# Reordering the convolution chunk on TensorE and splitting the bias out of the low-rank matmul, in an eight-core S4 + mixture-of-LoRA layer

## The reference

```python
x = _layernorm(x + s4(x))      # s4: causal convolution along the 4096 features, plus D*x
x = _layernorm(x + ffn(x))
# ffn:
base_out  = einsum('bsi,oi->bso', x, W) + b
gates     = softmax(einsum('bsi,ei->bse', x, Wr))
proj_r    = einsum('bsi,eri->bser', x, A)
lora_out  = einsum('bser,eor->bseo', proj_r, Bm)
out       = base_out + einsum('bse,bseo->bso', gates * 2.0, lora_out)
```

## Time and profile before

| | us |
|---|---|
| median of 2 runs | 1901.37 |
| the two runs | 1819.21 and 1983.53 |
| the profiled execution | 1824.94 |
| its span, core 1, the slowest | 1823.9 |
| spans of all cores | 1786.8 to 1823.9 |
| TensorE matmul busy | 1368.1 (75%) |
| ScalarE, VectorE busy | 298.3, 354.3 |

### The profile page before, as it was taken

The page is one execution under the profiler, slowest core; times in us unless marked ns, Lnnn a source line. Parts: engine busy times, 40 slices in busy tenths (PEclk is TensorE's granted clock), DMA queues, the critical chain, the costliest instruction groups (busy, mean ns, idle before and its releaser), DMA issues.

```text
span 1823.9 us, 15473 instructions; the slowest of 8 cores (1786.8 to 1823.9 us)
## 1 busy us (share of the span) xinstructions
PE 1368.1 (75%) x5820; PEld 558.2 (31%) x5820; DVE 354.3 (19%) x608; ACT 298.3 (16%) x588; POOL 58.8 (3%) x82
## 2 busy tenths in 40 slices
PE   0155547529978767678999996799999687999960
PEld 0024531103333322122444431234444122444420
DVE  2331000033000000516100041531000506200025
ACT  0032326200000000550000035200000550000000
POOL 3000001000000000000000000000000000000000
PEclk9999999857989888897999998799999997999985
DMA  4101024960999994162625405163452152734204
GB/s 84 15 5 12 1 13 55 195 165 1 201 207 204 209 204 128 24 208 102 267 92 202 121 1 148 83 253 139 162 172 59 24 208 76 247 139 161 116 1 184
DMA packets 72911, 222.81 MB, mean 122 GB/s; under 512 B 10820, under 2 KB 60068, under 8 KB 68453
## 3 DMA queue, kind: packets, MB, share of 16 engines
q0 software_dynamic: 58528, 154.10, 35.6%
q1 hardware_dynamic: 14310, 67.73, 9.7%
HBM read 205.32 MB, written 67.43 MB: 150 GB/s over the span
## 4 chain that ended last, share of the span: by engine, by line
PE 60%; DMA 13%; DVE 9%; another core or an unknown queue 7%; ACT 5%; issue 4%; POOL 1%; SPq 0%; DVEq 0%; ACTq 0%; POOLq 0%
PE ps L974 42%; DMA wtb<-WT 7%; DMA uTb<-uT 2%; PE ps L979 2%; ACT r1b L110 2%; DVE nt L105 2%; DVE r1b L105 2%; PE ps L906 1%; DVE bnbuf L105 1%; DMA o<-outf 1%; PE ps L810 1%; PE ps L841 1%; PE ps L848 1%; PE ps L854 1%
## 5 line engine op out<-in xcount | busy, mean ns | idle before, releaser
L974 PE MATMUL ps<-wtb,r1b 128*128 128x512 bf16 x3968 | 897.5, 385 | 60.2 <-DVE wtb L105 60.2
L974 PEld LDWEIGHTS ps<-wtb,r1b 128*128 128x128 bf16 x3968 | 382.8, 99 | 542.7 <-issue 115.3
L110 ACT CAST scr<-ps 128x512 bf16<-128x512 f32 x64 | 37.5, 586 | 968.5 <-PE ps L979 801.4
L105 DVE CAST scr<-ps 128x512 bf16<-128x512 f32 x64 | 44.3, 691 | 572.1 <-PE ps L979 568.7
L105 DVE BATCH_NORM_STATS2 bnbuf<-scr 128x6 f32<-128x512 bf16 x128 | 88.8, 694 | 13.8 <-DVE scr L105 0.7
L110 ACT ACTIVATE uTb<-r1b 128x512 bf16<-128x512 bf16 x128 | 80.6, 629 | 12.8 <-ACT r1b L110 1.5
L110 ACT CAST r1b<-ps 128x512 bf16<-128x512 f32 x128 | 75.0, 586 | 43.7 <-PE ps L856 34.4
L810 PE MATMUL ps<-r1b,onescb 128*1 128x512 bf16 x64 | 24.7, 386 | 74.0 <-DMA uTb<-uT 38.7
L105 DVE TENSOR_TENSOR wtb<-wtb,eyeb 128x128 bf16<-128x128 bf16 x32 | 7.2, 225 | 360.3 <-DMA wtb<-WT 357.5
L938 PE MATMUL ps<-wtb,r1b 128*128 128x512 bf16 x128 | 53.8, 587 | 27.2 <-DVE r1b L105 27.2
L105 DVE TENSOR_SCALAR outf<-scr,bnagg,sigcol 128x1024 f32<-128x1024 bf16 x64 | 52.0, 813 | 111.1 <-DMA o<-outf 108.9
(11 more groups left out here) (597 smaller groups left out, 827.9 us busy)
## 6 DMA issues: line engine op xcount, KB each, us to landing
wtb<-wscr POOLq DMA_DIRECT2D x24, 4096.0 KB, 15.4
wtb<-WT POOLq DMA_DIRECT2D x8, 4096.0 KB, 46.7
wscr<-wtb SPq DMA_DIRECT2D x8, 4096.0 KB, 19.0
o<-outf SPq DMA_DIRECT2D x64, 512.0 KB, 2.8
uTb<-uT POOLq DMA_DIRECT2D x16, 1024.0 KB, 14.5
g<-cvb_re POOLq DMA_DIRECT2D x1, 1024.0 KB, 7.3
g<-cvb_im POOLq DMA_DIRECT2D x1, 1024.0 KB, 10.2
catb<-CatA POOLq DMA_DIRECT2D x1, 288.0 KB, 9.0
```

Of the source, the lines that this page charges most:

```text
L105: t = sy.inc("V", fn(*a, **kw))
L110: t = sy.inc("S", fn(*a, **kw))
L974: T.matmul(ps[bi][0:128, 0:512], r1b[:, it * TT + tb * 128: it * TT + (tb + 1) * 128], wtb[par][:, it * 512:(it + 1) * 512], start=(it == ...
```

## The change

Three edits. (1) In the convolution, the carry-dependent matmuls (`pstat` and both uses of `wout_sb`) go to the end of a chunk's group and wait there for the carry copy of the chunk before; the carry's bank alternates between ps4 and ps5 (`pcb`). (2) The four matmuls for the sums are no longer spread over the next chunk: `st_mm(c-1)` issues them in one piece behind chunk c, behind a wait for all four ScalarE results. (3) The bias is taken out of the 33-row matmul: it becomes a matmul of its own (1 row of ones by 512 elements of `biasrb2`) in front of a 32-row one, and `sprojb` lies in the tile `nt`.

```diff
-    BmTd = dti("BmTd", [33, D4])
+    BmTd = dti("BmTd", [32, D4])
...
+        tk_bb = gdma("GS", biasrb2[0:1, :], biasd.ap())
         gdma("GS", onesrb[0:1, :], onesrd.ap())
...
-        sproj2 = sb("sproj2", [33, TT], BF16)
-        sprojb = sproj2[0:32, 0:TT]
+        sprojb = nt[0:32, 0:TT]
-        t_onerow = vch(V.memset, sproj2[32:33, :], 1.0)
...
+            def st_mm(c_):
+                evA, sqA, evB, sqB = stat_dep[c_]
+                deps = [evA, evB, sqA, sqB]
+                sy.waits("T", deps)
+                for k2 in range(2):
+                    mm1 = T.matmul(ps[6][0:1, 0:512], onescb[:, :], r1b[:, dsl],
+                    mm2 = T.matmul(ps[7][0:1, 0:512], onescb[:, :], uTb[:, ssl],
...
+                sy.waits("T", [bank_r.get(("psC", c % 2)), bank_r.get(pcb)])
+                T.matmul(ps[pcb][0:128, 0:512], win_sb[:, 0:128], uTb[:, slA], start=True, stop=False)
+                T.matmul(ps[pcb][0:128, 0:512], win_sb[:, 128:256], uTb[:, slB], start=False, stop=False)
...
+                sy.waits("T", [cv_prev])
+                cmt = sy.inc("T", T.matmul(ps[pcb][0:128, 0:512], pstat[:, :], carry[cur][:, :], start=False, stop=True))
...
                 if c > 0:
-                    st_part(c - 1, 3)
+                    st_mm(c - 1)
...
-                    sy.waits("T", [t_sp, t_onerow])
+                    T.matmul(ps[bi][0:128, 0:512], onesrb[0:1, :],
+                             biasrb2[0:1, os * 512:(os + 1) * 512], start=False, stop=False)
+                    sy.waits("T", [t_sp])
                     lm = T.matmul(ps[bi][0:128, 0:512],
-                                  sproj2[0:33, tb * 128:(tb + 1) * 128],
-                                  bmtb[0:33, os * 512:(os + 1) * 512], start=False, stop=True)
+                                  sprojb[:, tb * 128:(tb + 1) * 128],
+                                  bmtb[:, os * 512:(os + 1) * 512], start=False, stop=True)
```

More of the change, by code:

```diff
@@ L137, in build_nc @@
         ft = sb("ft", [64, 448], F32)
+        biasrb2 = sb("biasrb2", [1, D4], BF16)
         onesrb = sb("onesrb", [1, 128], BF16)
@@ L151, in build_nc @@
         gdma("GS", onescb[:, :], onescd.ap())
+        tk_bb = gdma("GS", biasrb2[0:1, :], biasd.ap())
         gdma("GS", onesrb[0:1, :], onesrd.ap())
-        t_bB = sy.tok("GS")
+        t_bB = tk_bb
         tk_setup = sy.tok("GS")
@@ L690, in build_nc @@
         catb = sb("catb", [128, NCH * 36], BF16)
-        bmtb = sb("bmtb", [33, D4], BF16)
-        sproj2 = sb("sproj2", [33, TT], BF16)
+        bmtb = sb("bmtb", [32, D4], BF16)
         eyeb = sb("eyeb", [128, 128], BF16)
@@ L800, in build_nc @@
             stats_fin = [None, None]
-            def st_part(c_, part):
+            def st_mm(c_):
                 evA, sqA, evB, sqB = stat_dep[c_]
                 first, last = (c_ == 0), (c_ == 15)
[L805 to L817, removed]
+                deps = [evA, evB, sqA, sqB]
+                if first:
+                    deps += [bank_r.get(6), bank_r.get(7)]
+                sy.waits("T", deps)
+                for k2 in range(2):
+                    dsl = slice((2 * c_ + k2) * TT, (2 * c_ + k2 + 1) * TT)
+                    ssl = slice(((2 * c_ + k2) % 16) * TT, ((2 * c_ + k2) % 16 + 1) * TT)
                     mm1 = T.matmul(ps[6][0:1, 0:512], onescb[:, :], r1b[:, dsl],
-                                   start=False, stop=last)
-                    if last:
+                                   start=(first and k2 == 0), stop=(last and k2 == 1))
+                    mm2 = T.matmul(ps[7][0:1, 0:512], onescb[:, :], uTb[:, ssl],
+                                   start=(first and k2 == 0), stop=(last and k2 == 1))
+                    if last and k2 == 1:
                         stats_fin[0] = sy.inc("T", mm1)
[L822 to L828, removed]
+                        stats_fin[1] = sy.inc("T", mm2)
+                    elif k2 == 1:
+                        stats_fin[0] = sy.inc("T", mm2)
+            cv_prev = None
             for c in range(16):
@@ L832, in build_nc @@
                 biA, biB = c % 2, 2 + c % 2
+                pcb = 4 + c % 2
                 slA = slice(((2 * c) % 16) * TT, ((2 * c) % 16 + 1) * TT)
@@ L855, in build_nc @@
                 T.matmul(ps[biB][0:128, 0:512], band0b[:, :], uTb[:, slB], start=False, stop=False)
+                sy.waits("T", [cv_prev])
+                cmt = sy.inc("T", T.matmul(ps[pcb][0:128, 0:512], pstat[:, :], carry[cur][:, :], start=False, stop=True))
+                bank_w[("psC", c % 2)] = cmt
+                amt = sy.inc("T", T.matmul(ps[biA][0:128, 0:512], wout_sb[:, 0:128], carry[cur][:, :], start=False, stop=True))
+                bank_w[biA] = amt
                 bmt = sy.inc("T", T.matmul(ps[biB][0:128, 0:512], wout_sb[:, 128:256], carry[cur][:, :], start=False, stop=True))
@@ L858, in build_nc @@
                 if c > 0:
-                    st_part(c - 1, 3)
+                    st_mm(c - 1)
                 sy.waits("S", [cmt, bank_r.get("carrynxt%d" % nxt)])
-                cv = sch(S.copy, carry[nxt][:, :], ps[4][0:128, 0:512])
-                bank_r["psC"] = cv
-                bank_r[4] = cv
+                cv = sch(S.copy, carry[nxt][:, :], ps[pcb][0:128, 0:512])
+                bank_r[("psC", c % 2)] = cv
+                bank_r[pcb] = cv
                 bank_r["carrynxt%d" % nxt] = cv
+                cv_prev = cv
                 sy.waits("S", [amt, bmt])
@@ L881, in build_nc @@
                     t_sc2 = ln2_scal(t_vc2)
-            for _p in range(4):
-                st_part(15, _p)
+            st_mm(15)
             t_s1 = stats_fin[0]
@@ L1021, in _host_prep @@
         np.asarray(inputs["L0_ffn_Wr"], dtype=f32).T], axis=1))
-    BmTh = np.ascontiguousarray(np.concatenate([
-        np.asarray(inputs["L0_ffn_Bm"], dtype=f32).transpose(0, 2, 1).reshape(32, D4),
-        np.asarray(inputs["L0_ffn_b"], dtype=f32).reshape(1, D4)], axis=0))
+    BmTh = np.ascontiguousarray(
+        np.asarray(inputs["L0_ffn_Bm"], dtype=f32).transpose(0, 2, 1).reshape(32, D4))
     biash = np.ascontiguousarray(np.asarray(inputs["L0_ffn_b"], dtype=f32))
```

## The result

The changed kernel takes 1841.18 us in the median of 11 runs, the kernel before 1819.2 in the median of 10. Each of the two series holds one run in a slower state of the chip (1960.08 and 1983.53 us), and such runs are left out of every ratio and of every mean over timed runs in this document. The ratio is 1.0127, with a 95% interval of 1.0105 to 1.0149: slower by 23 us, give or take 4. The forecast was 1840.0 for the time and +15.1 us for the difference. The time fits and the difference does not: its base, the profiled execution of 1824.94 us, was some 6 us above what the kernel before usually takes, and the sum was short by 8. That the total came within 1.2 us is luck: the high base made up for the short sum.

A forecast was written before the change was run, and what follows sets the result against it. TensorE bounds later tiles' streams, float32 weight loads tile 0's, a TensorE-ScalarE loop with input stops the convolution. Bias +20.3 and +1.6, setup +0.6, order -7.4 sum to +15.1 on 1824.9: 1840.0 us, range 1822 to 1856.

The forecast's parts named there:

- Bias matmul in tiles 1 to 3: Streams of later tiles: 93 token blocks each pay 0.218 us for the added matmul, all on the path, +20.3 us.
- Rival A: Added matmul pays an unhidden weight load at both neighbours, 0.31 us a block, giving 1849 us; chance 0.20.
- rival B: Only the 33-row shape costs 0.1 us each side, so the split-off bias is free, giving 1818 us; chance 0.07.
- Bias matmul in tile 0: Tile 0's stream: weight loads hide the added matmuls of os 1 to 6; os 0 and os 7 pay, +1.6 us.
- failed cover: Tile 0's stream, if weight loads hide none of the added matmuls: 31 x 0.218 = 6.8 us.
- The order in tile 0: Tile 0's convolution: chunks 1 to 4 and chunk 8 go faster and the first weight blocks are queued earlier, -2.4 us.
- The order in tiles 1 to 3: Convolutions: gains count only from chunk 8, partly lost to a colder clock; -1 in tile 1, -2 each in tiles 2, 3.
- The landing of quarter 3: Convolution input load lands 8.6 us after issue, while ScalarE needs 10.7 us for chunks 9 to 11, so stays hidden.
- rival D: Convolution order is worth nothing: quarter 3 comes late after faster chunks 9 to 11, end goes cold; +22.5, 1847 us; chance 0.11.
- a sign of being wrong: In the convolution: the forecast is wrong if quarter 3 holds chunk 12 for over 1 us.
- The setup: Before the first tile: one more load on GpSimd's queue delays ScalarE's first instruction, +0.6 us.
- The base: The profiled execution of the kernel before, 1824.9 us, to which the forecast difference of +15.1 us was added.

## Why the prediction was right or wrong

**Bias matmul in tiles 1 to 3: right.** 20.3 forecast; the streams add 6.5, 6.6 and 6.9 us, 20.0. The step from the 1-row to the 32-row matmul is 0.23 us. Rival A (0.31) and rival B (no changes of shape) are out: a block takes 7.55, and 128 to 1 and 32 to 128 rows pay 0.1 each like 128 to 33 did.

**Bias matmul in tile 0: the step that failed.** "The loads of blocks 3 to 7 run one after another and hide what os 1 to 6 gain in length" gave 1.6 us. The stages give 6.8 (2 to 12) and the timed runs 5 to 10, about the 6.8 that the prediction named for a failed cover. The terms that it gave to os 0 and os 7 fit: 0.5 (within its spread) and 0.9 us against 0.7 and 0.9. What failed is the zero for os 1 to 6: from the landing of block 2 to that of block 7 it takes 219.7 us where it took 214.3. The leads of the requests over the landing of the block ahead, which I had read as slack, did not shrink (blocks 4 to 7, mean over cores: 10.7, 4.8, 7.4 and 9.7 us in the eight executions without the matmul; 12.3, 6.0, 7.8 and 10.2 in the four with it), and the loads landed later instead. With four and eight matmuls part of the time is hidden after all, so "never hidden" is wrong too. Why a small addition is paid in full and a large one is not is open. In that stretch the same 44 MB moved with the DMA engines full in every execution, at 204.5 GB/s in the mean of the eight without, 199.6 with one, 197.3 with four and 196.2 with eight, so the same bytes took longer; whether the later requests did that, and how, was not tried.

**The order in tile 0: right up to the stream.** -2.4 forecast; from the first chunk to the first closing matmul the five executions with the new order have 156.2 us in the mean, the nine others 158.6, a gain of 2.4 give or take 2.3. That the loads of weights pass this gain on to the end of tile 0 is not shown: with the stream added, the four executions with the new order and no bias matmul have 459.7 us, the four of old order 459.2, with a spread of several us.

**The order in tiles 1 to 3: the mechanism right, the size too large.** -5 forecast, -1.5 to -2.5 measured (convolution -1.2 to -1.5 a tile, middle +0.6 to +0.9). The chunk of 3.57 us, the statistics that hold quarter 2, and chunk 8 at half clock were as told. Two terms were off. The landing of quarter 3 was taken from one row, 8.6 us; in the changed kernel's 24 loads it is 8.3 to 11.2 with 10 in the middle, and then it is late for chunk 12, as rival D had it: the wait is over 1 us in 19 of 24 convolutions, which the prediction had named as a sign of being wrong. And the end was given 0.5 us of clock in tiles 2 and 3, since core 1 went cold there already; most cores did not, and it costs 0.6 to 0.9 in the mean of all, which eats half of the rest. So the truth lies between the forecast and rival D.

**The setup: right where it starts, not seen where it ends.** +0.6 forecast; ScalarE's first instruction begins at 14.7 us in the mean over cores where it began at 13.9, and at 14.4 to 14.8 in the other kernels with the added load. The convolution of tile 0 begins at 260.2 us where it began at 262.8, 263.0 and 262.5, so what becomes of the 0.8 us can't be seen there. The added load is 8 KB, not the 16 that the prediction gave it.

**The base.** The sum was set on the time of one execution, 1824.94 us, some 6 above the median. Put on the stages: 20.0 + 6.8 - 2.4 - 2 = 22.4, which is what the ratio gives, 23 +- 4; and the two halves of the change timed apart, in the mean over cores, are 28.9 - 2.7 = 26.

## What to carry to other kernels

A wait that names the whole count of an engine waits for everything that engine was given, also for work on other buffers: here 28 us of statistics held a load they have nothing to do with, and taking that out is worth 27 us in the mean over cores, where the reordering is worth 3. Splitting a short contraction off a matmul costs a full pass of the moving columns, 0.22 us a token block here, while riding along as row 33 cost nothing that these runs show: a block is 7.33 us with it, and 7.55 - 0.23 = 7.32 with 32 rows and the split-off pass taken away. And in a stage bound by transfers, test the cover before counting on it, with several executions: "the queue is never empty" did not mean that added compute was hidden.

## What the runs showed of the hardware that I had not expected

The change between weights of different shape costs 0.09 to 0.10 us on each side whether the rows change (128 to 33, 128 to 1, 32 to 128) or the columns (128 to 1), and nothing between 1 and 32 rows (0.23 from start to start). The same 8 MB loads of weights by all eight cores make a stage that varies by 8 us in its mean over cores between three executions of one kernel (294.7 to 302.4), while the streams of the later tiles repeat within 0.6 us. And that the first added matmuls in that stage are paid in full and later ones in part (6.8, 15.7, 20.2 us for 6.8, 27, 53, the last from one execution that was the shorter of two) is unexplained.
